# A fused vision-transformer block on one core: the next group's routing one slot earlier, its gates one slot longer, and its last pooling slices spread over other slots

## What is computed

```
pooled = x.reshape(B, C, 14, 16, 14, 16).sum(axis=(3, 5))      # 196 tokens an image
h = einsum('bcij,ce->bije', pooled, channel_weights)           # 192 features
h = h + attention(layernorm(h), Wq, Wk, Wv)                    # one head
y = layernorm(h)                                               # then a mixture of 4 nested experts:
probs = softmax(y @ w_router.T); gate, idx = top_k(probs per expert, 98 of 196 tokens)
q, k, v, mlp = dispatched tokens @ w1 + b1                     # per image: 12 heads of 16
y2 = concat(gelu(mlp), softmax(q k / 4) v)
out = h + y + gate-weighted, masked (y2 @ w2 + b2)
```

## Time and profile before

| | us |
|---|---|
| three timed runs | 1763.33, 1766.48 (median), 1769.15 |
| the profiled execution's own time | 1757.22 |
| its span, first to last instruction | 1755.4 |
| PE busy in it | 1517.8 (86%) |
| DVE busy in it | 1218.5 (69%) |
| ACT busy in it | 847.3 (48%) |
| mean granted TensorE clock | 0.939 of full |

### The profile page before, as it was taken

One profiled execution on the slowest core, in us unless ns is written; L12 is line 12 of the kernel. 1 busy time (PEld: TensorE's weight loads), 2 busy tenths in 40 slices (PEclk: granted clock), 3 DMA queues, 4 the chain that ended last, 5 costly groups with the idle time before them and its releaser, 6 DMA issues.

```text
span 1755.4 us, 34644 instructions
## 1 busy us (share of the span) xinstructions
PE 1517.8 (86%) x12440; PEld 1258.9 (72%) x12440; DVE 1218.5 (69%) x2824; ACT 847.3 (48%) x1934; POOL 248.9 (14%) x319
## 2 busy tenths in 40 slices
PE   2146889898998999988998899989899989999998
PEld 2033778687786878777786777778687778878786
DVE  6658678757887578766887488765787677563552
ACT  0002555455554465454554555545554555546653
POOL 3021012200211002200111002300022002110000
PEclk9986889889999899998999899999899999989999
DMA  8985665516662475615673366706655152102220
GB/s 228 241 205 159 164 159 149 144 42 159 170 184 60 110 180 150 163 34 144 162 181 95 86 161 171 187 15 158 145 151 145 38 147 51 35 19 60 50 53 15
DMA packets 99574, 218.02 MB, mean 124 GB/s; under 512 B 61359, under 2 KB 75853, under 8 KB 88654
## 3 DMA queue, kind: packets, MB, share of 16 engines
q10 hardware_dynamic: 12032, 150.94, 32.4%
q1 hardware_dynamic: 87374, 64.88, 16.4%
HBM read 186.57 MB, written 28.90 MB: 123 GB/s over the span
## 4 chain that ended last, share of the span: by engine, by line
PE 50%; DVE 24%; issue 13%; DMA 7%; POOL 3%; ACT 2%; SPq 0%; DVEq 0%; POOLq 0%; ACTq 0%
PE bank L1050 12%; DVE psums L1258 9%; DVE peaks L1458 6%; PE bank L955 6%; PE bank L1019 5%; PE bank L985 5%; PE bank L1004 4%; DMA xt<-in_x_dram 4%; DMA qs<-shiftT 3%; PE bank L967 3%; POOL var L1590 2%; PE bank L878 2%; PE bank L1028 2%; PE bank L829 2%; PE bank L942 2%
## 5 line engine op out<-in xcount | busy, mean ns | idle before, releaser
L1458 DVE TENSOR_REDUCE peaks<-bank 98x2 f32<-98x392 f32 x768 | 423.3, 563 | 173.4 <-PE bank L985 152.7
L1207 ACT ACTIVATE Pb<-bank 98x392 f32<-98x392 f32 x768 | 374.5, 497 | 301.8 <-PE bank L1004 253.3
L1258 DVE TENSOR_REDUCE psums<-xt 112x2 f32<-112x512 f32 x672 | 425.8, 677 | 39.0 <-DMA xt<-in_x_dram 20.8
L1050 PE MATMUL bank<-w2T,hid 128*98 128x192 f32 x1536 | 312.1, 343 | 0.0
L985 PE MATMUL bank<-ks,qs 96*98 96x196 f16 x1536 | 269.3, 262 | 41.8 <-DVE peaks L1458 37.3
L1004 PE MATMUL bank<-qs,ks 97*98 97x196 f16 x1536 | 269.0, 259 | 23.3 <-DMA qs<-shiftT 21.5
L985 PEld LDWEIGHTS bank<-ks,qs 96*98 96x98 f16 x1536 | 166.1, 128 | 132.0 <-DVE peaks L1458 65.2
L1050 PEld LDWEIGHTS bank<-w2T,hid 128*98 128x98 f32 x1536 | 249.9, 176 | 3.6
L1004 PEld LDWEIGHTS bank<-qs,ks 97*98 97x98 f16 x1536 | 167.7, 130 | 35.4 <-DMA qs<-shiftT 24.4
L1019 PE MATMUL bank<-Pb,vals 98*32 98x196 f32 x3072 | 172.6, 343 | 1.2 <-ACT Pb L1207 1.2
L1618 POOL TENSOR_TENSOR fin<-fin,both 98x384 f32<-98x384 f32 x64 | 63.9, 998 | 728.8 <-DVE fin L1483 728.8
(11 more groups left out here) (185 smaller groups left out, 1777.9 us busy)
## 6 DMA issues: line engine op xcount, KB each, us to landing
xt<-in_x_dram ACTq DMA_DIRECT2D x94, 1568.0 KB, 9.0
qk_scratch<-qk SPq DMA_DIRECT2D x64, 294.0 KB, 4.1
qs<-qk_scratch SPq DMA_DIRECT2D x192, 73.5 KB, 3.0
ks<-qk_scratch SPq DMA_DIRECT2D x192, 73.5 KB, 3.1
out_dram<-fin SPq DMA_DIRECT2D x64, 147.0 KB
xt<-in_x_dram SPq DMA_DIRECT2D x2, 1568.0 KB, 15.3
qs<-shiftT SPq DMA_DIRECT2D x128, 2.3 KB
hid<-in_L_ffn_w_dram SPq DMA_DIRECT2D x1, 1440.0 KB
```

The lines of the kernel that those rows point to most:

```text
L1050: mm = pe.matmul(misc_ps[slot][0:HT, D * h:D * h + D], lhs, w2T[0:w, f, :], start=(f == 0), stop=(f == NF + 1))
L1207: act.activation(Pb[:, (H * i + h) % NP, :, :].rearrange("p a b -> p (a b)"), score_ps[s][0:HT, 0:2 * T], ACT.Exp, scale=float(DH) ** -0.5 ...
L1258: last = dve.tensor_reduce(psums[:, m % 2, t, 2 * p:2 * p + 2], v[:, 2 * p:2 * p + 2, :, :], AX.XY, ALU.add)
L1458: dve.tensor_reduce(peaks[:, h // 6, :, h % 6], peak_ps[s][0:HT, 0:2 * T].rearrange("p (q k) -> p q k", q=2), AX.X, ALU.max, negate=True). ...
```

## The change

- `TAKE` goes from 25 to 24: the whole of `routing` is one slot earlier. `wide` = 1 gives the gates more room: `gate_logits` half a slot, `gates`, `gate_rows` and `weigh` a slot later against `gate_scale`, so that `choose` still begins in slot 68.
- `chosen`, `spread` go from slot 85 to 86; the `turn_u`, `project` 0 and `stack` 0 by half a slot.
- Pooling of m = 3 ends by slot 18 in place of 20. The slices of the group after next may now lie in the slots from the end of `choose` plus 5 (89) to 95, which were quiet, and up to slot 101; slot 98 gets a third of its share (`few`). `own_row` ends and `planes` come later (`behind` 5).
- In the opening, an operation of the pooling is put in front of the slot's first `peak` and not at the slot's end.
- `planes` and `tok` of m = 2 leave the last slot of the body (and of the prologue) for slots 2 and 4 of the next body.

```diff
-def evenly(plan, count, first, end, quiet=(0, 0)):
-    room = [0 if quiet[0] <= k < quiet[1] else max(cost(TENSOR, plan[k]) - cost(VECTOR, plan[k]), 0.05)
+def evenly(plan, count, first, end, quiet=(0, 0), few=-1):
+    room = [0 if quiet[0] <= k < quiet[1] else max(cost(TENSOR, plan[k]) - cost(VECTOR, plan[k]), 0.05) / (1 + 2 * (k == few))
             for k in range(first, end)]
...
-def routing(dg, at):
+def routing(dg, at, wide=0):
...
-    ops += [(at, ("gate_scale", dg)), (at + 2, ("gate_logits", dg)), (at + 5, ("gates", dg)),
-            (at + 7, ("gate_rows", dg)), (at + 7.5, ("weigh", dg))]
-    at += 8
+    ops += [(at, ("gate_scale", dg)), (at + 2 + wide / 2, ("gate_logits", dg)), (at + 5 + wide, ("gates", dg)),
+            (at + 7 + wide, ("gate_rows", dg)), (at + 7.5 + wide, ("weigh", dg))]
+    at += 8 + wide
...
-    for slot, op in in_slots(pooling(1, 2, steadily(1, 0.24))):
-        plan[min(slot, len(plan) - 1)].append(op)
+    for slot, op in in_slots(pooling(1, AHEAD - 1, steadily(1, 0.24))):
+        if op[0] not in ("planes", "tok"):
+            plan[min(slot, len(plan) - 1)].append(op)
...
-TAKE = 25
+TAKE = 24
...
-    front, at = routing(1, TAKE)
+    front, at = routing(1, TAKE, 1)
...
-    quiet = (int(at), H * GRP)
-    at = rounds(plan, 1, int(at))
-    for slot, op in in_slots(choosing(1, at + 1) + turning(1, at + 4)):
+    began = int(at)
+    at = rounds(plan, 1, began)
+    quiet = (began, at + 5)
+    for slot, op in in_slots(choosing(1, at + 2) + turning(1, at + 4.5)):
...
-    at = evenly(plan, pieces * (GRP // PAIR - AHEAD), 0, TAKE - 4)
-    front = []
+    at = evenly(plan, pieces * (GRP // PAIR - AHEAD), 0, TAKE - 5)
+    front = [(2, ("planes", 1, AHEAD - 1)), (4, ("tok", 1, AHEAD - 1))]
...
-        at = evenly(plan, pieces * AHEAD, TAKE + 1, len(plan) - 3, quiet)
+        at = evenly(plan, pieces * AHEAD, TAKE + 1, len(plan) - 2, quiet, H * GRP + 2)
         for m in range(AHEAD):
-            front += pooling(2, m, at[pieces * m:])
+            front += pooling(2, m, at[pieces * m:], behind=5)
     for slot, op in in_slots(front):
-        plan[min(slot, len(plan) - 1)].append(op)
+        if op[0] in ("planes", "tok") and op[1:] == (2, AHEAD - 1):
+            continue
+        into = plan[min(slot, len(plan) - 1)]
+        peaks_at = [k for k, other in enumerate(into) if other[0] == "peak"]
+        into.insert(peaks_at[0] if slot >= H * GRP and peaks_at else len(into), op)
```

## The result

| | before | after |
|---|---|---|
| runs beside each other: median (lowest to highest), us | 1764.9 (1756.99 to 1769.15) | 1786.46 (1785.96 to 1787.61) |
| ratio to before, 95% interval | | 1.0131 [1.0096, 1.0166] |
| profiled execution: own time, span | 1757.22, 1755.4 | 1785.96, 1784.2 |
| PE busy in it | 1517.8 | 1512.8 |
| mean granted clock | 0.939 | 0.94 |

The kernel became 1.3% slower; the forecast was 55 us faster, and the time lies 44 us above the range. PE has 5 us less to do and 29 us more in which to do it, so PE idles more. In the lines cited of after, numbers are 6 higher than before (L985 is now L991, L1004 is L1010, L721 is L727, L1111 is L1117); in those of some kernels further down they are 7 or 3 higher. A wait of PE is given the slot in which ACT still is, so the `score` of slot 60 waits in slot 59.

The account below looks back on a forecast made before the run. PE bounds it (busy 1517.8 of 1755.4 us). Terms gave -10.1 us in each of loops 1 to 4, -7 each in loops 0 and 5, -1 in the pen, together -55 or -56: 1710 us, range 1686 to 1742.

Parts of the forecast that it names:

- (g): Slots 89 to 97: new wait for stack 0's loads, slowed by fetches in flight; +2.6 us a loop, bounds 0 and +5.
- Both fetches: Rival at slot 97: both fetches hold stack 0's loads, landing 2 to 4 us later; 1731 us, chance 0.13.
- slower: Rival: stack 0's loads in slot 97 wait for both fetches' end, 9 us late; 1774 us, chance 0.05.
- (a): Slot 99, opening: fewer pooling slices before `project` 2's subtraction, so PE's wait goes; -5.6 us, bounds -2.5 and -5.6.
- (b): Gates, slots 59 to 65: waits for the `shift` DMA and POOL go; -6.3 us, bounds -2.5 to -7.
- (c): Slots 94 and 95: `planes` and `tok` of m = 1 move there with nothing hiding them; +1.9 us.
- (d): Slots 100 to 103 and 0 to 11: opening's idle and low clock go; -2.1 us, bounds 0 and -2.1.
- (e): Slot 17: fetch moved from slot 11 to 10 ends a DMA wait; -1.1 us, bounds +0.6 and -1.1.
- (f): `chosen` a slot later, slots 84 to 88: PE works before waiting for the last `choose`; -1.0 us, between 0 and -2.5.
- (h): Slots 89 to 96: ten slices make DVE and ACT late; +0.4 us, bounds 0 and +1.2.
- (i): Slots 71 to 76, after the gates: clock may drop at waits for peaks; half of 2.3, +1.1 us.
- The rest of the routing moves ... 0: Routing elsewhere moves one slot, covered by PE's work, 0; if `norm1`'s wait for POOL lost cover, 2.9 us.

Follow-up runs that it names:

- the kernel with 1718: The changed kernel with slot 95's fetch in slot 98, `planes` and `tok` of m = 2 in slot 103, `norm1` half a slot later: 1718.06 us, 0.9779.
- the last kernel: The kernel with 1718, with the routing where the kernel before the change has it (`TAKE` 25, `wide` 0): 1727.71 us, 0.9805.

## Why the prediction was wrong, step by step

**(g) failed, and it decides.** Its computed arrival used the landing with one fetch in flight, 7.9 to 9.2 from the earlier trace rows, for a case with two. With one it was right: 6.7 to 7.9 and 7.7 to 8.4 in the experiments, and PE hardly waits. With two the last load took about 12.7 (998.68 to 1011.41). The write of `qk_scratch` took 4.1 us (991.15 to 995.31), as before. It cost 8.2 us a loop where 2.6 was forecast, 33 us more in the sum over six loops. "Both fetches" was a rival with 1731 and 0.13, and "slower" had this very mechanism with 0.05: if "the loads wait for the end of both fetches", they land "near 1005, 9 us late". Measured are 5.70 us of wait and 8.2 in slots 97 and 98, between the two. The text's own tests, a wait of over 4 us there and as many falls of the clock as before, both came out against it: loop 3 still has four falls, now in slots 2, 64, 72 and 97. The step had no row with two fetches, and then weighed its chances as though it had one.

The Trainium skill ("DMA: Bandwidth & Descriptors", section "Queues, rings and completion order") says that each DMA engine takes turns by packet between rows with work; from that I had that two fetches "would slow the loads no more than one does". The trace speaks against this reading: five of the six loads were issued before the second fetch, and the last three of the six landed at 1007.3, 1010.2 and 1011.4, around the second fetch's end at 1010.9. The first three, issued over 1.3 us ahead of the second fetch, landed in 7.3 to 7.7 as with one. The same section says that a completion's increment lands only after every earlier write of the same DMA engine, across its queues; that fits loads that are told complete about when a fetch is, but no run here tells it apart from plain sharing of bandwidth.

**(a) was right to 0.1 us**: 9.9 to 4.3, and alone on the kernel before the same. The step from the pen's slot 99 was a real bound.

**(b) was half right, and gave the gain to the wrong part.** `planes` and the `shift` no longer hold PE there, as said. But the run of the opening alone took these slots to 12.9, with the routing late and `planes` in slot 60: the earlier routing isn't needed for it, nor `planes` in slot 94. What these slots wait for there fits the last `own_row` standing ahead of the power. What the new places of the gates' steps brought were new waits. The wait of DVE for POOL was forecast at 1.2 us and came as 1.48, but its cover was misjudged. POOL, and DVE behind it, at the gates of loop 3:

```profile
941.47 2.90 POOL L1596 TENSOR_TENSOR var<-var,cst 98x16 f32<-98x16 f32 x1 [4.21 <-DVE var L1362]
```

```profile
944.41 0.23 DVE L1368 TENSOR_TENSOR soft<-lg,var 98x64 f32<-98x64 f32 x1 [1.48 <-POOL var L1596]
```

Behind the wait DVE has seven small operations of `gate_logits` before its next peak at 945.88, and PE, whose bank that peak frees, waits 1.99. I had counted PE's work against the wait alone and not the operation's own work behind it. With `gate_logits` in slot 62 and not 61, in the kernel with 1718, the window of loop 3 is 12.2 in place of 13.9. In the pen, which never had the old waits, the new one is a plain loss of 1.8: its 11.40 was no bound for the new order.

**(c) was right**: +1.9, slots 94 and 95 at full clock.

**(d) failed.** It saw the two operations as a cost that only moves. They were cover: for ACT's 1.28 us table load before slot 0, and with the stall of 1.66 came a lower clock, for 3.4 to 6.8 us in four bodies and 13.7 in loop 4 and the pen (0.62 over the pen's slots 0 to 11). Not all of that is shown to be the stall's: before has 3.4 us of it in slot 3 of loops 2 to 4, and loop 0 of after has 13.7 without the stall. And the fetch of slot 102 went to 103, beside a `shift`. Forecast 10 us saved in all, measured 10 lost.

**(e) failed in its sum.** The wait of 1.09 went, but the waits for peaks grew, in slot 12 from 0.66 to 1.25 and in slot 19 from nothing to 0.82. For the second, the step had called the fifth slice of slot 17 "hidden because the peak that needs them is two slots on"; DVE does the five in one piece, and the peak at 859.97 behind them is the one that PE waits for until 860.59. So +0.9 for -1.1:

```profile
857.00 3.06 DVE L1264 TENSOR_REDUCE psums<-xt 112x2 f32<-112x512 f32 x5 [0.22 <-DVE peaks L1464]
859.97 0.56 DVE L1464 TENSOR_REDUCE peaks<-bank 98x2 f32<-98x392 f32 x1
```

**(f), (h) and (i)** were within 0.8 us each: slots 84 to 88 -1.6, 89 to 93 +1.2, slots 71 to 76 +0.9. For (f), the 2.80 of slot 85 became 0.79 + 1.34 in loop 3. In (i) the +0.9 is a mean of 0 in two loops and 1.3 and 2.2 in two, a clock that falls or doesn't, as the step had it. No run takes (h) apart.

**"The rest of the routing moves ... 0" failed**: +1.9 in slots 25 to 28 of all seven bodies, 13.2 us. The step named the risk and its price of 2.9, and then compared the wrong slots. What counts is PE's work from the start of POOL's power to `norm1_turn`. Before, it started at 861.96 and PE came to the transpose at 865.73; after, it started at 872.39 and PE was there at 873.21 + 1.14 = 874.35. POOL of before and of after, then PE of before and the last that PE of after did ahead of it:

```profile
861.96 2.91 POOL L1590 TENSOR_TENSOR var<-var,cst 98x16 f32<-98x16 f32 x1 [7.80 <-DVE var L1291]
```

```profile
872.39 2.91 POOL L1596 TENSOR_TENSOR var<-var,cst 98x16 f32<-98x16 f32 x1 [6.73 <-DVE var L1297]
```

```profile
865.73 0.36 PE L847 MATMUL bank<-cst,x_tok 98*128 98x98 f32 x2
```

```profile
873.21 1.14 PE L1056 MATMUL bank<-w2T,hid 128*98 128x192 f32 x6
```

Before, 3.8 us of PE lay between, since slot 29 holds `norm_back`, `residual` and a `mix` ahead of `norm1_turn`; in slot 28 none of them is, 2.0 us are left, and 2.9 of POOL and 0.65 of DVE have to pass. Against this, slots 29 to 58 gained 1.2 that I had not in the sum.

Put together for seven bodies, measured less forecast: (g) +33, (d) +20, (b) +17, norm1 +13, (e) +10, (h) +5, the rest -15 (slots 29 to 58, (f), (i)): 83 us, the distance from -55 to +29.

## What to carry to other kernels

Small DMAs on which the busiest engine waits need the count of big transfers in flight at their issue and behind it; a landing measured with one in flight says nothing of two. An operation that only moves may be the cover of something on another engine (here a table load and a power): before moving it, look at who is idle just then, and count the work between the start of what is covered and the first who needs it. And in a plan made by fractions of a slot, one changed number moves operations that nobody named, and another moves none; compare the two plans operation by operation before reading a time. When several parts change at once, a gain in one place can belong to another part: the gates' came with the pooling slices.

## What the runs showed of the hardware that I had not expected

- Loads of 73.5 KB landed in 2.5 to 3.5 us in loop 3 with 196 KB fetches around them, in 6.7 to 8.9 over six loops behind one of 1568 KB (up to 9.2 in the earlier trace rows), and in 7.3 to 13.1 (14.7 in loop 0) with two. In loop 3 the fetches themselves took 11.9 and 13.4, against 11.0 for one alone with the same loads.
- A load issued just before a second fetch was no safer than one behind it: that of 997.07, 0.4 us ahead of the fetch, landed 13.1 us later. Those issued at least 1 us ahead landed in 7.3 to 8.5 in all six loops.
- The same wait for a `shift` in slot 17, with the fetch in slot 11, was 1.09 in loop 3 of before and 4.73 in loop 5 of the last kernel (3.78 in loop 5 of before). With a fetch just ahead, such waits vary from body to body. The runs of the last kernel spread over 10 us, and those of the kernel with 1718, which has no wait there, over 4; that the waits make the spread isn't shown.
